# Expert weights applied on the way out of PSUM, and result rows added to X by the DMA

## The chip, the cores and the metric

One core of one Trainium2 chip runs the whole program as one launch. The metric is the time of one execution on the device in microseconds (us), as the median over several runs. TensorE (PE, with PEld for its weight loads), VectorE (DVE), ScalarE (ACT), GpSimd (POOL) and the DMA queues of SyncE (SP), ACT and POOL work side by side and meet only at semaphores.

## The reference, cut to what matters

The program is four layers of cross attention and feed-forward over X, 2048 tokens (16 tiles of 128) of 256 numbers. The change touches the feed-forward of the first layer, a mixture of 32 experts with the 6 best for each token:

```
scores = softmax(xf @ gate_w.T)                       # 2048 x 32
top_w, top_i = top_k(scores, 6)
order = argsort(e_flat);  pos = place of the pair within its expert, valid = pos < 256
xbuf[buf_idx] = xf[t_s]                               # 32 experts x 256 places
h  = silu(xb @ w1) * (xb @ w3);   ob = h @ w2         # per expert
y[t_s] += ob[buf_idx] * w_s[:, None]                  # weight w_s = the pair's score
x = x + y + shared_experts(xn)
```

The next stage, the attention of the second layer, works on the sum, tile by tile.

## The kernel before

**Routing (`choose`, `slots`, `places`).** For four groups of four tiles DVE turns the logits into probabilities (`ex`, L1720 to L1727), picks the best eight of each row into `wts` (L1730, L1733), marks the chosen experts (`hit`, L1740) and works out each pair's place. The normalised tokens `xn` are stored to DRAM as `moe_in` (L1408, on SP's queue), one row of 256 numbers for each token. `token` holds, for each of the 8192 places, the row that belongs there (L1804).

**Experts (`MoeTop6.pe`, `.dve`, `.act`, `.pool`).** There is one iteration of a loop for each expert, in a software pipeline. In iteration e, TensorE turns the 256 tokens of expert e (`expert_in`, L1588), multiplies the turned tokens of expert e-1 by w1 and w3 (`expert_up`, L1602), and multiplies h of expert e-2 by w2 (`expert_down`, L1615), in that order. DVE runs `expert_product(e-1)` (L1829) and then `expert_copy(e-2)` (L1838), which moves the 128x512 result from PSUM to the tile `oe`; ACT stores `oe` to DRAM as `moe_out` (L1907). Between these, DVE and ACT split and centre the weights of the next stage (L1250 to L1273). The queue of POOL fetches the tokens of an expert with two indirect DMAs, one for each 128 places (L1923). The tile `xe` holds R = 3 experts; the gather of expert e waits until TensorE has turned expert e-3, and `expert_in(e)` waits on the landing of both gathers of its expert. SP loads the weights of later experts as TensorE lets go of their buffers (L1441, L1447, L1448), and pieces of the next stage's weights (L1194).

```
for e in range(N_EXP):                                  # POOL
    r = e % self.R
    if e >= self.R:
        g.wait_ge(self.p_xT.sem, self.p_xT.at(e - self.R + 1))
```

**Combining (`Combine`), inside the attention after it (`Fp8Attention`).** That stage runs in steps w, eight for each tile of 128 tokens. In each step every engine does its part of some heads: TensorE scores (L3229), projections (L3280, L3273), turns (L3208, L3216), values (L3240), output (L3261); DVE the maxima `f_nmax` (L3414), the sums of squares `f_hr` (L3399), the scaling of heads `f_raw` (L3409) and the rounding; ACT the exponentials (L3492) and, behind them in its order, the copies out of PSUM (`f_PT`, L3484); POOL the powers (L3579) and the division (L3573). `prepare` comes last in each step of DVE. For tile b, POOL gathers the six result rows of each token in steps -23+j to the tile's own zero (j = 0 to 5, L1134), each into its own tile `rows[:, j]`, and DVE adds them in six steps from -20+j (L1141), in steps 4 to 1 of the eight. The moments of the tile (`MOMENTS` = -14, L3328) wait for the sixth addition. A gather waits for the addition that emptied its tile, eight steps earlier.

Of the kernel before, what the change touches and what calls it, by code (L numbers as in the profile page):

```python
# [16 lines left out]
P = 128  # L17
# [84 lines left out]
class Core:  # L102


    def __init__(self, nc, ctx, A, out):
        self.nc, self.ctx, self.A, self.out = nc, ctx, A, out
        self.sig = Signals(nc, ctx)
        self.psum = ctx.enter_context(nc.psum_tensor("bank", [P, 8 * BANK], F32))
        self.bank = [self.psum[:, i * BANK:(i + 1) * BANK] for i in range(8)]
        self.X = self.sb("X", [P, B, D])  # L110
        self.ident = self.sb("ident", [P, P])
        self.ident16 = self.sb("ident16", [P, P], BF16)
        self.ones = self.sb("ones", [P, P])
        self.half_pow = self.sb("half_pow", [P, 2 * B])
        self.zero = self.sb("zero", [P, FILL])
        self.xbuf = nc.dram_tensor("moe_in", (B * P, D), F32, kind="Internal").ap()
        self.obuf = nc.dram_tensor("moe_out", (SLOTS + 1, D), F32, kind="Internal").ap()
        self.d_x = [self.sig.claim(f"d_x{g}", 1, 16, own=True) for g in range(4)]
        self.d_const = self.sig.claim("d_const", 2, 16, own=True)
        self.d_fill = self.sig.claim("d_fill", 1, 16, own=True)  # L120
        self.d_out = self.sig.claim("d_out", 4, 16, own=True)
        self.v_const = self.sig.claim("v_const", 3, own=True)
        self.s_stage = self.sig.claim("s_stage", 0, own=True)
        self.stages = 0
        sem = lambda n: self.sig.claim(n, 0, own=True).sem
        self.dve = Chain(nc.vector, sem("dve_order"))
        self.act = Chain(nc.scalar, sem("act_order"))
        self.pool = Chain(nc.gpsimd, sem("pool_order"))
# [986 lines left out]
class Combine:  # L1115


    def __init__(self, k):
        self.k = k

# [4 lines left out]
    def signals(self):  # L1125
        claim = self.k.sig.claim
        self.d_row = [claim(f"c_d_row{j}", B, 16, own=True) for j in range(TOP_K)]
        self.v_add = claim("c_v_add", B * TOP_K, own=True)

    def gather(self, g, rows, b, j):  # L1130
        if b:
            g.wait_ge(self.v_add.sem, self.v_add.at(TOP_K * (b - 1) + j + 1))
        at = bass.IndirectOffsetOnAxis(ap=self.slot[:, b, j:j + 1], axis=0)
        g.indirect_dma_start(rows[:, j, :], None, self.k.obuf, at, bounds_check=SLOTS, oob_is_err=False).then_inc(self.d_row[j].sem, 16)  # L1134

    def add(self, v, rows, b, j):
        X = self.k.X
        v.wait_ge(self.d_row[j].sem, self.d_row[j].at(b + 1))
        if j:
            v.wait_ge(self.v_add.sem, self.v_add.at(TOP_K * b + j))  # L1140
        v.scalar_tensor_tensor(X[:, b, :], rows[:, j, :], self.wts[:, b, j:j + 1], X[:, b, :], ALU.mult, ALU.add).then_inc(self.v_add.sem, 1)  # L1141


class Fp8Weights:
# [138 lines left out]
class MoeTop6(Stage):  # L1283
# [7 lines left out]
    NG = 4  # L1291
    GROUPS = B // NG
    SI = 2 * INTER
    R, R2 = 3, 4
    LEFT, HALF = INTER - P, P // 2
    W13 = 2 * P + HALF + INTER - P
    PLACES = (0, P), (HALF, HALF + INTER - P)
# [11 lines left out]
    def allocate(self):  # L1309
        k, NG = self.k, self.NG  # L1310
        s = lambda name, shape, dt=F32: k.sb(f"m_{name}", shape, dt, self.ctx)
        self.token = s("token", [P, TILES], U32)
        self.xe = s("xe", [P, self.R, 2, D])
        self.w13 = s("w13", [P, self.R, DC, self.W13])
        with ExitStack() as c:
            s = lambda name, shape, dt=F32: k.sb(f"m_{name}", shape, dt, c)
# [1 line left out]
            self.gate = s("gate", [P, DC, N_EXP])  # L1318
            self.tri, self.ones16, self.trif = s("tri", [P, P], BF16), s("ones16", [P, P], BF16), s("trif", [P, P])
            self.expert, self.slot0 = s("expert", [P, N_EXP]), s("slot0", [P, N_EXP])  # L1320
            self.ex, self.total = s("ex", [P, NG, N_EXP]), s("total", [P, N_EXP])
# [13 lines left out]
        with ExitStack() as c:  # L1335
# [4 lines left out]
        self.rows_in = k.xbuf.rearrange("(b p) d -> p b d", p=P)  # L1340
        self.rows_out = k.obuf[0:SLOTS, :].rearrange("(e s p) d -> e p s d", e=N_EXP, p=P)
        self.signals()

    def signals(self):
        claim, G = self.k.sig.claim, self.GROUPS
        self.d_par = claim("d_par", 6, 16)
        self.d_sw = claim("d_weights", 3, 16)
        self.d_rows = claim("m_d_rows", G, 16)
# [8 lines left out]
        self.d_xe = [claim(f"m_d_xe{r}", 2 * -(-(E - r) // self.R), 16, own=True) for r in range(self.R)]  # L1357
# [11 lines left out]
    def sp(self, sp):  # L1369
        if not self.before:  # L1370
            self.load_parameters(sp)
            for g in range(self.GROUPS - 1):
                self.store_rows(sp, g)
        for t in self.tail(0, 99):
            self.before.sp_step(sp, t)
        self.store_rows(sp, self.GROUPS - 1)
        self.fp8.load_parameters(sp)
        for e in range(self.R):
            self.load_up(sp, e)
        sp.wait_ge(self.v_dn.sem, self.v_dn.at(2 * self.GROUPS))  # L1380
# [27 lines left out]
        sp.dma_start(self.rows_in[:, bs, :], self.xn[:, bs, :]).then_inc(self.d_rows.sem, 16)  # L1408

    def sp_before(self, sp, t):
        if t == 0:
# [162 lines left out]
        x.then_inc(self.p_dn.sem, 1)  # L1576

    def expert_in(self, t, e):
        i, r = e % 2, e % self.R
        ps = self.k.bank[6 + i]  # L1580
        t.wait_ge(self.d_xe[r].sem, self.d_xe[r].at(2 * (e // self.R + 1)))
# [132 lines left out]
    def choose(self, v, g):  # L1714
# [12 lines left out]
        c.mark(v.scalar_tensor_tensor(e, e, FLT_MIN, e, ALU.is_ge, ALU.mult))  # L1727
        c.after()
        for i, b in enumerate(bs):
            c.mark(v.max(wts[:, b, :], self.ex[:, i, :]))  # L1730
        c.after()
        for i, b in enumerate(bs):
            c.mark(v.max_index(self.topi[:, b, :], wts[:, b, :], self.ex[:, i, :]))  # L1733
        c.after()
        c.mark(v.tensor_copy(self.topf[:, sl, :], self.topi[:, sl, :]))
        c.after()
# [94 lines left out]
                            ALU.mult).then_inc(self.v_he.sem, 1)  # L1831

    def expert_copy(self, v, e):
        i = e % 2
        v.wait_ge(self.p_ed.sem, self.p_ed.at(e + 1))
        if e >= 2:
            v.wait_ge(self.d_oe[i].sem, self.d_oe[i].at(e // 2))
        v.tensor_copy(self.oe[:, i, :, :].rearrange("p s d -> p (s d)"), self.k.bank[4 + i][:, :]).then_inc(self.v_oe.sem, 1)  # L1838

# [71 lines left out]
    def pool(self, g):  # L1911
# [1 line left out]
            self.pool_before(g, 3)  # L1913
        self.power(g, self.GROUPS - 1)
        g.wait_ge(self.v_token.sem, self.v_token.at(1))
        g.wait_ge(self.d_rows.sem, self.d_rows.at(self.GROUPS))
        for e in range(N_EXP):
            r = e % self.R
            if e >= self.R:
                g.wait_ge(self.p_xT.sem, self.p_xT.at(e - self.R + 1))  # L1920
            for s_ in range(2):
                at = bass.IndirectOffsetOnAxis(ap=self.token[:, 2 * e + s_:2 * e + s_ + 1], axis=0)
                g.indirect_dma_start(self.xe[:, r, s_, :], None, self.k.xbuf, at, bounds_check=B * P - 1,  # L1923
                                     oob_is_err=False).then_inc(self.d_xe[r].sem, 16)

    def power(self, g, n):
# [1121 lines left out]
class Fp8Attention(Stage):  # L3048
# [274 lines left out]
    def prepare(self, v, w):  # L3323
# [1 line left out]
        c = self.k.dve  # L3325
        b = self.batch(w, self.MOMENTS)
        if b is not None:
            v.wait_ge(self.combine.v_add.sem, self.combine.v_add.at(TOP_K * (b + 1)))  # L3328
            self.moments(v, b, self.k.X[:, b, :])
        b = self.batch(w, self.SECOND)  # L3330
        if b is not None:
# [250 lines left out]
def program(nc, A, out, stages=range(8)):  # L3582
    with ExitStack() as ctx:
# [14 lines left out]
        if 1 in stages:  # L3598
            with ExitStack() as memory:
# [5 lines left out]
                with ExitStack() as rest:  # L3605
                    if first:
                        first.allocate_tail(rest)
                        spare = k.sb("spare", [P, 5120], F32, rest)
                    experts.allocate()
                    if first:  # L3610
                        flat = lambda x, dims: x.rearrange(f"p {dims} -> p ({dims})")
                        first.allocate_within(Space(flat(fp8.cut_w[:, :, :, :], "m c n").bitcast(F32), spare[:, :], flat(fp8.wkv[:, :, :], "c n"),
                                                    flat(experts.xe[:, :, :, :], "r s d")))
# [152 lines left out]
```

## Time and profile before

| | us |
|---|---|
| median of 3 runs | 2259.33 (2258.38 to 2268.91) |
| the profiled execution, its own time | 2274.26 |
| its span | 2272.5 |
| expert loop, first and last turn of tokens | starts 407.7 and 575.4 |
| attention of the second layer, in its regular part | 720 to 1280 |

The profiled execution lies 14.9 us above the median. "Busy" is the time in which an engine worked on an instruction; the releaser in square brackets is what ended an engine's idle time. Landing is the time from the issue of a DMA until its semaphore is complete.

### The profile page before, as it was taken

To read this page: it belongs to the slowest core of one execution; us is meant where nothing else is said; L and a number is where in the kernel's file an instruction comes from. 1 tells how busy PE (TensorE), PEld (TensorE's weight loads), DVE (VectorE), ACT (ScalarE), POOL (GpSimd) and SP (SyncE) were. 2 spreads that over 40 slices of the span, in tenths; PEclk is the share of its full clock that TensorE was granted. 3 is DMA by queue.
4 is the path that set the end of the run, shared out by engine and by line. 5 is a ranking of instruction groups with operands and counts; after the bars stand their busy time and mean duration, and the time that the engine had idled before them with its cause. 6 is when DMAs were issued, how large, how long until landed. Compare 5 with 4: busy or idle time off the path is not lost. (4 is left out here: it accounts for less than half of the span.)

```text
span 2272.5 us, 41321 instructions
## 1 busy us (share of the span) xinstructions
PE 1915.8 (84%) x12949; PEld 1178.3 (52%) x12949; DVE 1763.4 (78%) x4155; ACT 1355.3 (60%) x3511; POOL 959.4 (42%) x1253
## 2 busy tenths in 40 slices
PE   5999889999678999999999998598588566888888
PEld 3444355666356666666666675465244133333335
DVE  4899758464579999999999988665686797888845
ACT  0777721343168888888888886132266564577753
POOL 4444200443376566665566543232874121343210
PEclk7899859999889999999999999699599776799979
DMA  6577520678230000000001001542797310577610
GB/s 147 145 179 180 129 91 1 198 246 260 73 61 20 17 20 22 20 20 22 17 20 22 10 4 47 181 139 81 206 259 201 96 35 21 134 187 184 166 39 38
DMA packets 258319, 223.63 MB, mean 98 GB/s; under 512 B 36601, under 2 KB 237916, under 8 KB 257852
## 3 DMA queue, kind: packets, MB, share of 16 engines
q1 hardware_dynamic: 234812, 179.24, 28.8%
q0 software_dynamic: 12240, 32.39, 5.5%
q10 hardware_dynamic: 11056, 9.38, 1.3%
q8 instruction: 110, 1.80, 0.3%
q14 instruction: 101, 0.83, 0.1%
HBM read 142.50 MB, written 79.32 MB: 98 GB/s over the span
## 5 line engine op out<-in xcount | busy, mean ns | idle before, releaser
L3579 POOL TENSOR_TENSOR f_hr<-f_hr,half_pow 128x4 f32<-128x4 f32 x192 | 215.4, 1122 | 192.1 <-DVE f_hr L3399 191.6
L966 ACT ACTIVATE a_PT<-bank 128x512 f32<-128x512 f32 x384 | 214.7, 604 | 84.5 <-PE bank L720 77.6
L852 DVE TENSOR_REDUCE a_nm<-bank 128x2 f32<-128x512 f32 x384 | 243.2, 683 | 25.6 <-PE bank L713 24.2
L3492 ACT ACTIVATE f_Pm<-bank,f_nmax 128x128 f32<-128x128 f32 x512 | 183.6, 391 | 100.0 <-DVE f_nmax L3414 99.7
L713 PE MATMUL bank<-a_stack_k,a_stack_q 57*128 57x256 bf16 (+1 forms) x768 | 165.0, 300 | 80.1 <-DVE a_nm L852 45.3
L3280 PE MATMUL bank<-f_cut_w,f_zc 128*128 128x512 f16 x768 | 202.5, 388 | 14.0 <-DVE f_raw L3409 7.8
L3573 POOL TENSOR_TENSOR f_Pm<-f_Pm,f_rs 128x512 f32<-128x512 f32 x128 | 142.6, 1114 | 111.9 <-DVE f_rs L3419 111.9
L3409 DVE TENSOR_TENSOR f_raw<-bank,f_hr 128x512 f32<-128x512 f32 x192 | 131.3, 684 | 60.1 <-POOL f_hr L3579 59.4
L966 ACT ACTIVATE f_cut_w<-bank 128x512 f32<-128x512 f32 x256 | 141.7, 600 | 51.6 <-PE bank L720 41.0
L852 DVE TENSOR_REDUCE spare<-bank 128x2 f32<-128x512 f32 x256 | 162.4, 681 | 8.8 <-PE bank L713 7.4
L720 PE MATMUL bank<-a_stack_q,a_stack_k 60*128 60x256 bf16 (+1 forms) x768 | 157.7, 290 | 4.4 <-ACT a_PT L966 4.1
L3504 ACT ACTIVATE f_cb<-bank,f_rsmooth 128x128 bf16<-128x128 f32 x512 | 153.7, 431 | 5.2 <-PE bank L3240 3.5
L3216 PE MATMUL bank<-ident,f_raw 128*128 128x128 f32 x768 | 114.8, 277 | 42.4 <-ACT f_PT L3484 41.3
L713 PEld LDWEIGHTS bank<-a_stack_k,a_stack_q 57*128 57x128 bf16 (+1 forms) x768 | 59.4, 100 | 175.4 <-DVE a_nm L852 112.8
L3399 DVE TENSOR_REDUCE f_hr<-f_sq 128x4 f32<-128x516 f32 x192 | 131.2, 683 | 20.8 <-ACT f_sq L3527 20.6
L3527 ACT ACTIVATE f_sq<-bank 128x512 f32<-128x512 f32 x192 | 121.1, 631 | 43.8 <-PE bank L3273 22.1
L1923 POOL DMA_INDIRECT m_xe<-moe_in,m_token x64 | 73.6, 1150 | 168.3 <-DVE m_token L1804 81.9
L3229 PEld LDWEIGHTS bank<-f_KT,f_QT 128*128 128x128 f32 x1024 | 131.1, 194 | 20.7 <-issue 11.8
L3229 PE MATMUL bank<-f_KT,f_QT 128*128 128x128 f32 x1024 | 136.9, 277 | 0.3 <-ACT f_Pm L3492 0.3
L3240 PE MATMUL bank<-f_PT,f_Vv 128*128 128x256 f32 x512 | 132.1, 380 | 1.2 <-ACT f_cb L3504 1.2
L3273 PE MATMUL bank<-f_wkv,f_cT 128*128 128x512 f32 x256 | 123.2, 606 | 6.2 <-DMA f_cT<-in_ctx_T 5.9
L3216 PEld LDWEIGHTS bank<-ident,f_raw 128*128 128x128 f32 x768 | 91.3, 142 | 69.3 <-issue 55.9
(417 smaller groups left out, 4960.1 us busy)
## 6 DMA issues: line engine op xcount, KB each, us to landing
o<-a_sums SPq DMA_DIRECT2D x32, 512.0 KB, 4.2
cut<-a_parts SPq DMA_DIRECT2D x64, 192.0 KB, 3.9
cut<-a_parts SPq DMA_DIRECT2D x96, 128.0 KB, 3.2
m_w<-in_w SPq DMA_DIRECT2D x32, 368.0 KB, 4.6
moe_out<-m_oe ACTq DMA_DIRECT2D x32, 256.0 KB
cut<-spare SPq DMA_DIRECT2D x32, 192.0 KB, 3.5
cut<-spare SPq DMA_DIRECT2D x48, 128.0 KB, 2.6
spare<-cut SPq DMA_DIRECT2D x32, 192.0 KB, 3.6
```

The lines of the kernel that those rows point to most:

```text
L713: x = t.matmul(ps[:, n * D:(n + 1) * D], self.stack_q[rows, i, slot, n * P:(n + 1) * P], self.stack_k[rows, i, slot, :], start=True, stop= ...
L720: x = t.matmul(ps[:, n * D:(n + 1) * D], self.stack_k[rows, i, slot, n * P:(n + 1) * P], self.stack_q[rows, i, slot, :], start=True, stop= ...
L852: v.tensor_reduce(self.nm[:, g % 2, :, at % self.J, at // self.J], self.k.bank[h % 3][:, :].rearrange("p (n m) -> p n m", n=2), AX.X, ALU. ...
L966: a.activation(self.PT[:, h % 8, :, :].rearrange("p m n -> p (m n)"), self.k.bank[3 + h % 3][:, :], ACT.Exp).then_inc(self.a_exp.sem, 1)
L3216: x = t.transpose(ps[:, h * P:(h + 1) * P], self.raw[:, n % self.NRAW, h * HD1:(h + 1) * HD1], self.k.ident[:, :])
L3229: x = t.matmul(ps[:, j * P:(j + 1) * P], self.QT[:, cross, h, :], self.KT[:, cross, h // 2, :], start=True, stop=True)
L3240: x = t.matmul(self.k.bank[7][:, j * 2 * P:(j + 1) * 2 * P], self.Vv[:, cross, n * 2 + j, :], self.PT[:, u % 2, j * 2 * P:(j + 1) * 2 * P] ...
L3280: x = t.matmul(ps[:, :], self.zc[:, b % 2, j, c_, :], self.fp8.cut_w[:, m, c_, at:at + BANK], start=(m == 0 and c_ == 0), stop=(m == 1 and ...
L3492: x = a.activation(self.Pm[:, i, j * P:(j + 1) * P], ps[:, j * P:(j + 1) * P], ACT.Exp, bias=self.nmax[:, i, j:j + 1], accum_out=self.rs[: ...
L3504: x = a.activation(self.cb[:, u % self.NCB, j * P:(j + 1) * P], ps[:, j * P:(j + 1) * P], ACT.Copy, scale=self.fp8.rsmooth[:, h:h + 1])
L3573: g.tensor_tensor(pm, pm, self.rs[:, u % 3, :].unsqueeze(2).to_broadcast([P, self.HPB, P]), ALU.mult).then_inc(self.g_P.sem, 1)
L3579: g.tensor_tensor(f, f, self.k.half_pow[:, 0:self.HPB], ALU.pow).then_inc(self.g_hr.sem, 1)
```

## The change

- A second DRAM tensor, `moe_weighed`, has rows of 256 + 32 numbers: the token and its 32 probabilities. The tokens are stored to its first 256 columns; the probabilities are kept in a tile `prob`, and SP stores them to the last 32 with four DMAs (`store_prob`), each of which waits for `hit` of its group. These stand on SP's queue after the first three `load_up` and before its wait for the shared experts.
- The gathers of the tokens fetch rows of 288 numbers. The tile `xe` holds RX = 4 experts, and the gather of expert e waits for `expert_copy(e-4)`, which reads the weights from that tile.
- `expert_copy` is a multiplication by the weight of each place, broadcast over 256 columns.
- Tiles b = 0 and 1 (`PLAIN`) are still gathered to `rows` and added by DVE, now without a weight (`tensor_tensor`). For b = 2 to 15 the indirect DMA adds to X itself (`compute_op=ALU.add`), each after the landing of the one before, and DVE issues nothing; the moments wait for the landing of the sixth.
- `xe` and `spare` change size, and the first attention's tiles are laid over them in another order.

```diff
     def gather(self, g, rows, b, j):
-        if b:
-            g.wait_ge(self.v_add.sem, self.v_add.at(TOP_K * (b - 1) + j + 1))
         at = bass.IndirectOffsetOnAxis(ap=self.slot[:, b, j:j + 1], axis=0)
-        g.indirect_dma_start(rows[:, j, :], None, self.k.obuf, at, bounds_check=SLOTS, oob_is_err=False).then_inc(self.d_row[j].sem, 16)
+        if b < self.PLAIN:
+            if b:
+                g.wait_ge(self.v_add.sem, self.v_add.at(TOP_K * (b - 1) + j + 1))
+            g.indirect_dma_start(rows[:, j, :], None, self.k.obuf, at, bounds_check=SLOTS, oob_is_err=False).then_inc(self.d_row[j].sem, 16)
+            return
+        if j:
+            g.wait_ge(self.d_row[j - 1].sem, self.d_row[j - 1].at(b + 1))
+        g.indirect_dma_start(self.k.X[:, b, :], None, self.k.obuf, at, bounds_check=SLOTS, oob_is_err=False,
+                             compute_op=ALU.add).then_inc(self.d_row[j].sem, 16)
 
     def add(self, v, rows, b, j):
         X = self.k.X
+        if b >= self.PLAIN:
+            return
...
-        v.scalar_tensor_tensor(X[:, b, :], rows[:, j, :], self.wts[:, b, j:j + 1], X[:, b, :], ALU.mult, ALU.add).then_inc(self.v_add.sem, 1)
+        v.tensor_tensor(X[:, b, :], X[:, b, :], rows[:, j, :], ALU.add).then_inc(self.v_add.sem, 1)
+
+    def wait(self, v, b):
+
+        done = (self.v_add, TOP_K * (b + 1)) if b < self.PLAIN else (self.d_row[TOP_K - 1], b + 1)
+        v.wait_ge(done[0].sem, done[0].at(done[1]))
...
+    def store_prob(self, sp, g):
+        bs = slice(self.NG * g, self.NG * (g + 1))
+        sp.wait_ge(self.v_hit.sem, self.v_hit.at(g + 1))
+        sp.dma_start(self.prob_in[:, bs, :], self.prob[:, bs, :]).then_inc(self.d_rows.sem, 16)
...
     def expert_copy(self, v, e):
-        i = e % 2
+        i, weight = e % 2, self.xe[:, e % self.RX, :, D + e:D + e + 1]
...
-        v.tensor_copy(self.oe[:, i, :, :].rearrange("p s d -> p (s d)"), self.k.bank[4 + i][:, :]).then_inc(self.v_oe.sem, 1)
+        v.tensor_tensor(self.oe[:, i, :, :], self.k.bank[4 + i][:, :].rearrange("p (s d) -> p s d", s=2),
+                        weight.to_broadcast([P, 2, D]), ALU.mult).then_inc(self.v_oe.sem, 1)
...
         g.wait_ge(self.v_token.sem, self.v_token.at(1))
-        g.wait_ge(self.d_rows.sem, self.d_rows.at(self.GROUPS))
+        g.wait_ge(self.d_rows.sem, self.d_rows.at(2 * self.GROUPS))
         for e in range(N_EXP):
-            r = e % self.R
-            if e >= self.R:
-                g.wait_ge(self.p_xT.sem, self.p_xT.at(e - self.R + 1))
+            r = e % self.RX
+            if e >= self.RX:
+                g.wait_ge(self.v_oe.sem, self.v_oe.at(e - self.RX + 1))
             for s_ in range(2):
                 at = bass.IndirectOffsetOnAxis(ap=self.token[:, 2 * e + s_:2 * e + s_ + 1], axis=0)
-                g.indirect_dma_start(self.xe[:, r, s_, :], None, self.k.xbuf, at, bounds_check=B * P - 1,
+                g.indirect_dma_start(self.xe[:, r, s_, :], None, self.k.weighed, at, bounds_check=B * P - 1,
                                      oob_is_err=False).then_inc(self.d_xe[r].sem, 16)
...
-            v.wait_ge(self.combine.v_add.sem, self.combine.v_add.at(TOP_K * (b + 1)))
+            self.combine.wait(v, b)
```

## Rows read from the trace of the kernel before

**Rows 1.** The page, part 1: busy time of each engine over the span.
```profile
PE 1915.8 (84%) x12949; PEld 1178.3 (52%) x12949; DVE 1763.4 (78%) x4155; ACT 1355.3 (60%) x3511; POOL 959.4 (42%) x1253
```
**Rows 2.** Busy time by stretch: stretch, its length, engines, granted clock, DMA share, GB/s.
```profile
480.00:530.00 50.00, 50.00 (x219) 34.54 (x218) 31.39 (x43) 21.18 (x36) 22.82 (x19) 1.00 0.80 246
720.00:1200.00 480.00, 442.21 (x2714) 324.05 (x2713) 439.17 (x1113) 400.58 (x1323) 297.17 (x277) 1.00 0.08 20
```
**Rows 3.** Timeline of the expert loop: start, duration, engine, line.
```profile
482.00 0.66 PE L1588 MATMUL bank<-ident,m_xe 128*128 128x128 f32 x4
...
484.74 1.45 POOL L1923 DMA_INDIRECT m_xe<-moe_in,m_token  x1 [0.30 <-issue]
...
487.50 0.66 PE L1588 MATMUL bank<-ident,m_xe 128*128 128x128 f32 x4
...
487.60 0.69 DVE L1838 COPY m_oe<-bank 128x512 f32<-128x512 f32 x1 [1.44 <-PE bank L1615]
...
488.92 1.50 POOL L1923 DMA_INDIRECT m_xe<-moe_in,m_token  x1 [2.74 <-PE bank L1588]
...
490.73 0.99 POOL L1923 DMA_INDIRECT m_xe<-moe_in,m_token  x1 [0.30 <-issue]
```
**Rows 4.** Source line L1923: all its gathers, then two single ones.
```profile
L1923 POOL DMA_INDIRECT m_xe<-moe_in,m_token x64: 992/998/1502, 402.7 to 561.6; - x64
...
DMA to landing us min/median/max: 2.8/4.7/8.3
...
L1923 POOL DMA_INDIRECT m_xe<-moe_in,m_token x1: 998/998/998, 446.8 to 446.8; - x1
...
DMA to landing us min/median/max: 5.6/5.6/5.6
...
L1923 POOL DMA_INDIRECT m_xe<-moe_in,m_token x1: 994/994/994, 556.6 to 556.6; - x1
...
DMA to landing us min/median/max: 4.9/4.9/4.9
```
**Rows 5.** Timeline of TensorE in the attention, tile after tile: the starts after a gap.
```profile
905.08 0.63 PE L3216 MATMUL bank<-ident,f_raw 128*128 128x128 f32 x4 [0.59 <-ACT f_PT L3484]
...
917.17 1.06 PE L3216 MATMUL bank<-ident,f_raw 128*128 128x128 f32 x8 [1.24 <-ACT f_PT L3484]
...
929.89 0.63 PE L3216 MATMUL bank<-ident,f_raw 128*128 128x128 f32 x4 [0.35 <-ACT f_PT L3484]
...
937.65 1.05 PE L3261 MATMUL bank<-f_wproj,f_cb 128*128 128x256 bf16 x8 [1.06 <-DVE f_raw L3409]
...
942.74 0.63 PE L3216 MATMUL bank<-ident,f_raw 128*128 128x128 f32 x4 [0.54 <-ACT f_PT L3484]
...
953.55 0.63 PE L3216 MATMUL bank<-ident,f_raw 128*128 128x128 f32 x4 [0.59 <-ACT f_PT L3484]
```
**Rows 6.** Timeline of VectorE in the same stretch.
```profile
913.44 0.48 DVE L1141 SCALAR_TENSOR_TENSOR X<-f_rows,wts,X 128x256 f32<-128x256 f32 x1
913.84 0.68 DVE L3414 TENSOR_REDUCE f_nmax<-bank 128x4 f32<-128x512 f32 x1
...
920.62 0.69 DVE L3399 TENSOR_REDUCE f_hr<-f_sq 128x4 f32<-128x516 f32 x1 [0.36 <-ACT f_sq L3527]
```
**Rows 7.** Source line L1134: the gathers of result rows, ns, and their landing.
```profile
L1134 POOL DMA_INDIRECT f_rows<-moe_out,slot x96: 994/1092/1253, 592.9 to 1265.0; - x96
...
DMA to landing us min/median/max: 2.8/3.0/4.3
```
**Rows 8.** Groups by line, VectorE: a product that reads PSUM.
```profile
L1819 DVE TENSOR_TENSOR X<-X,bank 128x512 f32<-128x512 f32 x5 | 3.3, 683 | 4.4 <-PE bank L1574 4.4
```
**Rows 9.** Source line L1740, which writes `hit`: first and last start.
```profile
L1740 DVE TENSOR_REDUCE m_hit<-m_hot x4: 1445/1450/1486, 311.7 to 376.5; 128x128 bf16<-128x768 f32 x4
```
**Rows 10.** Busy time by stretch in two later attentions, columns as in rows 2.
```profile
1680.00:1700.00 20.00, 16.49 (x138) 8.55 (x137) 17.38 (x35) 11.24 (x24) 14.10 (x22) 0.83 0.93 260
1980.00:2000.00 20.00, 16.86 (x214) 8.26 (x214) 17.45 (x38) 15.77 (x34) 8.89 (x18) 1.00 0.76 178
```

More of the change, by code:

```diff
@@ L116, in __init__ @@
         self.xbuf = nc.dram_tensor("moe_in", (B * P, D), F32, kind="Internal").ap()
+        self.weighed = nc.dram_tensor("moe_weighed", (B * P, D + N_EXP), F32, kind="Internal").ap()
         self.obuf = nc.dram_tensor("moe_out", (SLOTS + 1, D), F32, kind="Internal").ap()
@@ L1115 @@
 class Combine:
+    PLAIN = 2
     def __init__(self, k):
@@ L1127, in signals @@
         self.d_row = [claim(f"c_d_row{j}", B, 16, own=True) for j in range(TOP_K)]
-        self.v_add = claim("c_v_add", B * TOP_K, own=True)
+        self.v_add = claim("c_v_add", self.PLAIN * TOP_K, own=True)
     def gather(self, g, rows, b, j):
-        if b:
-            g.wait_ge(self.v_add.sem, self.v_add.at(TOP_K * (b - 1) + j + 1))
         at = bass.IndirectOffsetOnAxis(ap=self.slot[:, b, j:j + 1], axis=0)
-        g.indirect_dma_start(rows[:, j, :], None, self.k.obuf, at, bounds_check=SLOTS, oob_is_err=False).then_inc(self.d_row[j].sem, 16)
+        if b < self.PLAIN:
[7 more added lines that the diff above has]
+                             compute_op=ALU.add).then_inc(self.d_row[j].sem, 16)
     def add(self, v, rows, b, j):
         X = self.k.X
+        if b >= self.PLAIN:
+            return
         v.wait_ge(self.d_row[j].sem, self.d_row[j].at(b + 1))
@@ L1293 @@
     SI = 2 * INTER
-    R, R2 = 3, 4
+    R, R2, RX = 3, 4, 4
     LEFT, HALF = INTER - P, P // 2
@@ L1312, in allocate @@
         self.token = s("token", [P, TILES], U32)
-        self.xe = s("xe", [P, self.R, 2, D])
+        self.xe = s("xe", [P, self.RX, 2, D + N_EXP])
         self.w13 = s("w13", [P, self.R, DC, self.W13])
@@ L1320, in allocate @@
             self.expert, self.slot0 = s("expert", [P, N_EXP]), s("slot0", [P, N_EXP])
-            self.ex, self.total = s("ex", [P, NG, N_EXP]), s("total", [P, N_EXP])
+            self.ex, self.total, self.prob = s("ex", [P, NG, N_EXP]), s("total", [P, N_EXP]), s("prob", [P, B, N_EXP])
             self.topi, self.topf, self.ntop = s("topi", [P, B, 8], U32), s("topf", [P, B, 8]), s("ntop", [P, B, 2])
@@ L1339, in allocate @@
             self.he, self.sge, self.oe = s("he", [P, 2, 2, CAP]), s("sge", [P, 2, 2, CAP]), s("oe", [P, 2, 2, D])
-        self.rows_in = k.xbuf.rearrange("(b p) d -> p b d", p=P)
+        weighed = k.weighed.rearrange("(b p) d -> p b d", p=P)
+        self.rows_in, self.prob_in = weighed[:, :, 0:D], weighed[:, :, D:D + N_EXP]
         self.rows_out = k.obuf[0:SLOTS, :].rearrange("(e s p) d -> e p s d", e=N_EXP, p=P)
@@ L1347, in signals @@
         self.d_sw = claim("d_weights", 3, 16)
-        self.d_rows = claim("m_d_rows", G, 16)
+        self.d_rows = claim("m_d_rows", 2 * G, 16)
         self.v_hot, self.p_who, self.v_who, self.v_token = claim("m_v_hot", G), claim("m_p_who", G + 1), claim("m_v_who", G), claim("m_v_token", 1)
@@ L1356, in signals @@
         E = N_EXP
-        self.d_xe = [claim(f"m_d_xe{r}", 2 * -(-(E - r) // self.R), 16, own=True) for r in range(self.R)]
+        self.d_xe = [claim(f"m_d_xe{r}", 2 * -(-(E - r) // self.RX), 16, own=True) for r in range(self.RX)]
         self.d_w13 = [claim(f"m_d_w13_{r}", -(-(E - r) // self.R), 16) for r in range(self.R)]
@@ L1379, in sp @@
             self.load_up(sp, e)
+        for g in range(self.GROUPS):
+            self.store_prob(sp, g)
         sp.wait_ge(self.v_dn.sem, self.v_dn.at(2 * self.GROUPS))
@@ L1578, in expert_in @@
     def expert_in(self, t, e):
-        i, r = e % 2, e % self.R
+        i, r = e % 2, e % self.RX
         ps = self.k.bank[6 + i]
-        t.wait_ge(self.d_xe[r].sem, self.d_xe[r].at(2 * (e // self.R + 1)))
+        t.wait_ge(self.d_xe[r].sem, self.d_xe[r].at(2 * (e // self.RX + 1)))
         if e < 2:
@@ L1726, in choose @@
         c.after()
-        c.mark(v.scalar_tensor_tensor(e, e, FLT_MIN, e, ALU.is_ge, ALU.mult))
+        c.mark(v.scalar_tensor_tensor(self.prob[:, sl, :], e, FLT_MIN, e, ALU.is_ge, ALU.mult))
         c.after()
-        for i, b in enumerate(bs):
-            c.mark(v.max(wts[:, b, :], self.ex[:, i, :]))
+        for b in bs:
+            c.mark(v.max(wts[:, b, :], self.prob[:, b, :]))
         c.after()
-        for i, b in enumerate(bs):
-            c.mark(v.max_index(self.topi[:, b, :], wts[:, b, :], self.ex[:, i, :]))
+        for b in bs:
+            c.mark(v.max_index(self.topi[:, b, :], wts[:, b, :], self.prob[:, b, :]))
         c.after()
@@ L3607, in program @@
                         first.allocate_tail(rest)
-                        spare = k.sb("spare", [P, 5120], F32, rest)
+                        spare = k.sb("spare", [P, 4096], F32, rest)
                     experts.allocate()
@@ L3611, in program @@
                         flat = lambda x, dims: x.rearrange(f"p {dims} -> p ({dims})")
-                        first.allocate_within(Space(flat(fp8.cut_w[:, :, :, :], "m c n").bitcast(F32), spare[:, :], flat(fp8.wkv[:, :, :], "c n"),
-                                                    flat(experts.xe[:, :, :, :], "r s d")))
+                        first.allocate_within(Space(flat(fp8.cut_w[:, :, :, :], "m c n").bitcast(F32), flat(experts.xe[:, :, :, :], "r s d"),
+                                                    spare[:, :], flat(fp8.wkv[:, :, :], "c n")))
                         plan.append(first)
```

## The prediction, made before the changed kernel ran

> **What bounds the kernel now.** I read the page's busy table first: TensorE is busy for 84% of the span and VectorE for 78% [rows 1], so neither is the bound everywhere, and each stage has to be read by itself. The change works in two. The view of busy time by stretch shows the expert loop with TensorE busy for 50.00 of 50 us at the full clock, VectorE for only 31.39, and the DMA engines at 0.80 [rows 2]: TensorE alone sets the time there, and everything else has slack as long as it arrives on time. In the attention after it TensorE is busy for 442.21 of 480 us and VectorE for 439.17 [rows 2]; the two share the bound, and the timeline says who waits for whom. In the eight steps that one tile takes, behind the gap at 905.08, TensorE stands still five times, 1.24 + 0.35 + 1.06 + 0.54 + 0.59 = 3.8 us in all, four times for a copy of ScalarE and once for VectorE [rows 5]. ScalarE's copies stand behind exponentials that wait for VectorE's maxima, and the maxima come straight after the addition that closes VectorE's step (913.44, then 913.84) [rows 6]. So additions on VectorE do reach TensorE, in this stage only.
>
> **Part 1, the additions leave VectorE: a gain.** There are 16 x 6 = 96 additions of 0.48 us [rows 6]; 14 of 16 tiles lose theirs, 84 in all. The instruction behind one starts 0.40 us after it (913.44 to 913.84) [rows 6], so what is freed is 84 x 0.40 = 33.6 us, or 2.4 us for each tile. How much of this reaches the end I take from the gaps [rows 5]. The addition at 913.44 delays the maxima of the step with the 1.24 gap: 0.40 back. The next one stands in a step where VectorE is ahead and waits 0.36 for ScalarE at 920.62 [rows 6]: nothing back. The third stands before the gap of 0.35: 0.35 back. The fourth and fifth stand before 1.06 and 0.54: 0.40 each. The sixth is followed by a step without a gap, but VectorE's lead is carried to the gap of 0.59: I give it half, 0.2. That is 1.7 us for each tile, 14 x 1.7 = **-24 us**. The ends are -33.6 (all of it; the gaps, 3.8, would hold it) and 0 (TensorE finds another late partner each time). The twelve additions that stay lose their weight operand and keep their time.
>
> **Part 2, the DMA adds.** POOL issues the same 96 indirect DMAs, 1.09 us each [rows 7]. New is that gathers j = 1 to 5 of 14 tiles, 70 in all, wait for the landing of the one before. They are issued one step apart, and a tile takes 953.55 - 905.08 = 48.5 us (the same wait, one tile apart) [rows 5], a step an eighth of it, 6.1 us. A plain gather lands in 3.0 us, at most 4.3 [rows 7]. An adding one isn't in the trace; from both sides, 3.0 (no dearer) and twice that, 6.0 (it reads X as well), both end within a step. Behind the waiting gather on POOL's queue stand the next step's power and division, which VectorE and TensorE need, so beyond 6.1 us it would hurt; up to there it costs nothing. Its moments are taken four steps after the sixth gather: hidden by 24 us.
>
> **Part 3, the expert's tokens are fetched later: a loss.** Before, the gather of expert e was let go by the turning of expert e-3, three iterations ahead. Now it waits for `expert_copy(e-4)`. `expert_down(e-4)` is the last work of iteration e-2, so the copy runs at the start of iteration e-1, and only that one iteration lies between the gather's release and `expert_in(e)`. There are four buffers, but the release comes two iterations later. Working it out:
> - One iteration is 487.50 - 482.00 = 5.50 us [rows 3].
> - The copy runs from 487.60 to 488.29; the turning that releases POOL today ends at 488.16. So POOL starts 0.1 later than now. It now starts its second gather at 490.73, 3.23 after the iteration's start [rows 3]; that becomes 3.33.
> - The second gathers of this phase, ten from 446.8 (5.6 us) to 556.6 (4.9 us), have a median landing of 4.9 [rows 4].
> - Landed: 3.33 + 4.9 = 8.2 us after the end of iteration e-2, where 5.5 would do. TensorE waits 2.7 us.
> - The phases alternate. In the other one the second gather starts at 484.74, 2.74 after the start [rows 3]; with the 0.1 and the median of all landings, 4.7 [rows 4], it is in after 7.5 us. Two iterations then take the longer of 5.5 + 8.2 = 13.7 and 5.5 + 7.5 = 13.0, against 11.0 now. So the gap of 2.7 falls once in two experts, and the other gather has 0.7 to spare.
> - Twelve pairs (experts 8 to 31): 12 x 2.7 = 32.4. One of them meets the 2 MB load of the next stage, where a landing takes up to 8.3 [rows 4]: 3.4 more. Experts 4 to 7 have the short phase twice: 2 x (13.0 - 11.0) = 4.0. Sum **+40 us**.
>
> The ends: with the shortest landing, 2.8 [rows 4], the wait is 3.33 + 2.8 - 5.5 = 0.6, 14 times: +9. With 5.6 [rows 4] it is 3.4: 12 x 3.4 + 3.4 + 4 = +48. I stay at 4.9, since the gathers keep their place in the iteration and with it the loads and the store they share the engines with; rows of 288 numbers instead of 256 speak for more, the idle 2.7 us for less. The share of busy DMA, 0.80 now [rows 2], would go down by 11.0/13.7.
>
> A landing has a price in the Trainium skill too ("DMA: Bandwidth & Descriptors", section on the anatomy of one DMA on the gpsimd path): about 2.0 us plus the bytes at 436 GB/s, by which 147 KB would take an estimated 2.3 us, the wait would be 0.1 and the whole part some 2 us. By that, the trace disagrees under this load: the shortest of its 64 landings is 2.8, and those of this phase stand near 5.
>
> **Part 4, the rest, at nothing.** `expert_copy` reads PSUM with a second operand: 0.683 us for this size [rows 8] against 0.69 now [rows 3]. The four stores of probabilities stand on SP's queue ahead of its wait for the last shared addition, which VectorE issues after `hit` of the last group anyway, so they hold up nothing there. That `hit` is written at 376.5 + 1.45 = 378 [rows 9], 25 us before the first gather at 402.7 [rows 4]; this slack is the cover, and without it the first gather would be late by one landing, some 5 us. The new destinations of `choose` and the layout of the first attention change no instruction's size.
>
> **Sum.** -24 + 40 + 0 = +16 us. On the profiled execution's own time that is 2274.3 + 16 = 2290; it lies 14.9 above the median, and against the median of 2259.3 I forecast **2275 us**.
>
> **The rivals.**
> - *The gathers land early, not slower.* If landings in the loop come down to 2.8, the smallest of 64 [rows 4], because TensorE's waiting empties the queues, the loop loses 9 us and the attention gains 24 to 33.6: -15 to -25, some 2239. It decides at a landing of 3.9: 3.33 + 3.9 - 5.5 = 1.7, 14 x 1.7 = 24, the gain of part 1. For it speak that the gap comes before the iteration and thins the traffic; against it that the loads are issued at the same places in an iteration as before. The skill's page named above gives a like outcome by its price. Chance 0.14.
> - *The clock falls in the gaps.* In one later attention TensorE is busy for 16.49 of 20 us and has a mean granted clock of 0.83, so that it spends a third of the time at 1.2 GHz and the rest at 2.4, in another for 16.86 at 1.00, all at 2.4 [rows 10]. The expert loop would have 11.0 of 13.7, as low a share as these. At 0.83 its 28 iterations, 154 us, take 154/0.83 - 154 = 31 us more: +47, 2306. Chance 0.17.
> - *The freed VectorE brings nothing*, since ScalarE (400.58 of 480 [rows 2]) or the powers of POOL hold TensorE instead: +40, 2299. Chance 0.09.
> - *Adding DMAs land late.* At 8.3 us, the largest landing of any gather [rows 4], each of 70 waits holds POOL 2.2 us, 154 us; POOL is idle for 38% of the stage [rows 2] and would swallow about half, so +77 on top: 2352. Chance 0.06.
> - *It cancels*, the waits shrinking to 1.7 us a pair: 2259. Chance 0.12.
> - The forecast as worked out: 0.42, mostly between 2262 and 2292.
>
> **How the numbers follow.** A measurement of this kernel can tell about 0.5%, 11 us, from no change. Slower by more: two thirds of the forecast (0.29), most of the clock's fall (0.16), nothing freed (0.09), late adding (0.06), 0.60. Faster by more: nearly all of early landings, 0.13. Within: the rest, 0.27. The range leaves out the late adding and the outer part of early landings, and reaches to the clock's case: 2240 to 2312.
>
> **What would show it.** In the changed profile L1588 would wait for the DMA of the tokens some 14 times, 2 to 3 us each, and TensorE's share in 480 to 530 fall to about 0.8; POOL would wait for `expert_copy`, not for the turn. In the attention one tile would take 46.8 us instead of 48.5, L1141 stand 12 times, and TensorE's gaps be halved. Wrong would be: no wait at L1588 (part 3), a tile of 48 us or more (part 1), or POOL waiting for landings at L1134 (part 2).

## The result, and the profile after

The changed kernel takes 2315.0 us (median of 4 runs, 2304.0 to 2320.4) beside 2260.5 for the kernel before, also of 4 runs. The ratio of their runs is 1.0215, with a 95% interval of 1.0183 to 1.0248, which on 2260.5 is +49 us; the medians differ by 54.5. Medians and ratios, here and below, leave out executions in a slower state of the chip; the profile of the run with the late release alone is of one and is read for its expert loop only. The profiled execution took 2320.4 us, its span 2318.6, 46.1 more than before. Two source lines give the place: the turns of tokens, which stand once in every iteration of the expert loop, and the output additions of the attention, once in every second step (L1613 and L3470 of the changed kernel, L1588 and L3444 before): durations in ns, first and last start.

```profile
L1613 PE MATMUL bank<-ident,m_xe x128: 272/273/477, 406.1 to 637.3; 128*128 128x128 f32 x128
...
L3470 DVE SCALAR_TENSOR_TENSOR X<-bank,f_ws,X x64: 468/477/485, 763.8 to 1457.2; 128x256 f32<-128x256 f32 x64
```
The same rows of the kernel before:
```profile
L1588 PE MATMUL bank<-ident,m_xe x128: 272/273/473, 407.7 to 575.8; 128*128 128x128 f32 x128
...
L3444 DVE SCALAR_TENSOR_TENSOR X<-bank,f_ws,X x64: 470/473/485, 698.7 to 1409.0; 128x256 f32<-128x256 f32 x64
```

| part of the profiled span, us | before | after | |
|---|---|---|---|
| up to the first turn of tokens | 407.7 | 406.1 | -1.6 |
| expert loop, first to last turn | 168.1 | 231.2 | +63.1 |
| from there to the first output addition (run-in of the attention) | 122.9 | 126.5 | +3.6 |
| first to last output addition | 710.3 | 693.4 | -16.9 |
| the rest | 863.5 | 861.4 | -2.1 |
| span | 2272.5 | 2318.6 | +46.1 |

The loop loses 63 us and the attention gives back 13. Busy time by stretch, with the columns of [rows 2], for the changed kernel:

```profile
480.00:530.00 50.00, 41.47 (x158) 29.16 (x158) 21.49 (x29) 14.94 (x25) 13.98 (x13) 0.86 0.58 172
...
760.00:1240.00 480.00, 456.18 (x2807) 334.78 (x2807) 425.35 (x1082) 413.43 (x1364) 338.42 (x287) 1.00 0.13 21
```
Where [rows 2] has TensorE busy for 50.00 of 50 us at the full clock with 219 matmuls, it is now busy for 41.47, the mean granted clock is 0.86, so part of the stretch runs at 1.2 GHz, the lower of its two levels, and only 158 matmuls get done. In the attention TensorE's share has gone up, from 442.21 of 480 to 456.18. The waits of the loop (who waited for whom, total, times, longest) name the cause:

```profile
POOL m_xe L1949 <- DVE m_oe L1863: 151.6, 28, 10.4
...
PEld bank L1613 <- DMA m_xe<-moe_weighed,m_token: 46.4, 16, 5.8
...
PE bank L1613 <- DMA m_xe<-moe_weighed,m_token: 39.3, 15, 5.4
```
POOL stands ready and waits 28 times for the copy of a result, which is what lets go of a buffer now, and TensorE waits for the DMA that POOL then issues. The timeline shows one round of it, to be read beside [rows 3]:

```profile
520.79 1.11 PE L1613 MATMUL bank<-ident,m_xe 128*128 128x128 f32 x4 [2.80 <-DMA m_xe<-moe_weighed,m_token]
...
527.68 0.66 PE L1613 MATMUL bank<-ident,m_xe 128*128 128x128 f32 x4
527.79 0.69 DVE L1863 TENSOR_TENSOR m_oe<-bank,m_xe 128x512 f32<-128x512 f32 x1 [1.43 <-PE bank L1640]
...
529.25 1.24 POOL L1949 DMA_INDIRECT m_xe<-moe_weighed,m_token  x1 [7.27 <-DVE m_oe L1863]
530.79 1.00 POOL L1949 DMA_INDIRECT m_xe<-moe_weighed,m_token  x1 [0.30 <-issue]
...
535.91 0.66 PE L1613 MATMUL bank<-ident,m_xe 128*128 128x128 f32 x4 [2.67 <-DMA m_xe<-moe_weighed,m_token]
541.41 0.66 PE L1613 MATMUL bank<-ident,m_xe 128*128 128x128 f32 x4
```
The last two rows are one iteration without a wait, 5.50 us as before. The iteration from 527.68 to 535.91 holds a wait of 2.67: the second gather is issued at 530.79, lands 5.1 us later by the row of its source line, 535.9, and TensorE starts. From 520.79 to 527.68 there is no wait at all, yet the iteration takes 6.89: its four turns take 1.11 us in place of 0.66, which is TensorE at the lower of its two clock levels. So the 63 us are waits and clock. Busy time over the whole loop, before and after, gives a first division:

```profile
407.70:575.80 168.10, 166.26 (x720) 115.81 (x721) 89.98 (x148) 66.12 (x115) 69.50 (x61) 0.98 0.77 241
...
406.10:637.30 231.20, 191.90 (x720) 133.66 (x721) 87.97 (x148) 66.13 (x115) 64.65 (x61) 0.86 0.59 180
```
The same 720 matmuls keep TensorE busy for 25.6 us longer, and its idle time goes from 1.8 to 39.3 us, +37.5. The experiments have to show what causes either.

### The profile page after: what moved, and what is told of

Read it like the earlier page. It is cut to its first block and busy times, and to the rows that moved or that the text cites. A ratio compares the mean times of both kernels' runs of the same rounds, so it can differ in the third digit from the quotient of the medians.

```text
span 2318.6 us, 41171 instructions
## 1 busy us (share of the span) xinstructions
PE 1932.6 (83%) x12949; PEld 1195.2 (52%) x12949; DVE 1720.3 (74%) x4071; ACT 1354.7 (58%) x3511; POOL 997.6 (43%) x1253
## 3 DMA queue, kind: packets, MB, share of 16 engines
q0 software_dynamic: 20304, 33.44, 7.2%
## 5 line engine op out<-in xcount | busy, mean ns | idle before, releaser
L3605 POOL TENSOR_TENSOR f_hr<-f_hr,half_pow 128x4 f32<-128x4 f32 x192 | 221.7, 1155 | 160.8 <-DVE f_hr L3425 159.6
L1949 POOL DMA_INDIRECT m_xe<-moe_weighed,m_token x64 | 68.7, 1074 | 244.2 <-DVE m_oe L1863 151.6
L853 DVE TENSOR_REDUCE m_xe<-bank 128x2 f32<-128x512 f32 x256 | 162.2, 679 | 8.8 <-PE bank L714 7.2
L3553 ACT ACTIVATE f_sq<-bank 128x512 f32<-128x512 f32 x192 | 121.1, 631 | 45.5 <-PE bank L3306 22.7
L1143 POOL DMA_INDIRECT X<-moe_out,slot x84 | 137.4, 1636 | 21.3 <-issue 12.7
```

The source lines that it names most:

```text
L853: v.tensor_reduce(self.nm[:, g % 2, :, at % self.J, at // self.J], self.k.bank[h % 3][:, :].rearrange("p (n m) -> p n m", n=2), AX.X, ALU. ...
L1143: g.indirect_dma_start(self.k.X[:, b, :], None, self.k.obuf, at, bounds_check=SLOTS, oob_is_err=False, compute_op=ALU.add).then_inc(self.d ...
L3605: g.tensor_tensor(f, f, self.k.half_pow[:, 0:self.HPB], ALU.pow).then_inc(self.g_hr.sem, 1)
```

## The experiments

Theory A: the gather waits for `expert_copy(e-4)`, lands 2.7 us late for every second expert (some 40 us), and the clock falls because of the gaps (some 23 us). Rivals: the loop is slow because of what it computes and moves now (longer rows, a product in place of a copy); or the clock falls for a reason of its own. For the attention: the additions' relief, less what the adding DMAs cost on POOL, or nothing of that.

**One more token buffer.**
```diff
-    R, R2, RX = 3, 4, 4
+    R, R2, RX = 3, 4, 5
```


> The changed kernel with five token buffers instead of four, so that a gather is let go one iteration earlier. Theory A (the late release costs 40 us of waits and the clock's fall that follows from them 23 us): a gather has 11.0 us where it needs 8.2, the waits at the turning of tokens go, the granted clock in the loop is back at 1.00, the loop's turns span 168 us instead of 231, and the whole takes some 2315 - 63 = 2252 us, a little under the kernel before. Rival B (the longer rows of 288 numbers and the product with a broadcast weight slow the loop): the waits shrink at most in part and the kernel stays above 2290.

Measured: 2258.5 us (10 runs) beside 2262.2, ratio 0.9967 (0.9936 to 0.9998), 6 us above the 2252 that was expected. The loop spans 169.8 us, and busy time by stretch has it back:
```profile
480.00:530.00 50.00, 50.00 (x221) 34.72 (x220) 30.66 (x42) 23.03 (x38) 19.84 (x18) 1.00 0.82 245
```
TensorE is busy throughout at 2.4 GHz, and the DMA engines at 0.82 move the longer rows beside the rest. The wait at the turn of tokens shrinks from 39.3 us to 3.5, nearly what it was before (1.8). One buffer takes away waits and clock loss together, so both hang on the release; the longer rows and the product cost the loop 1.7 us at most (169.8 and 168.1).

**The waits filled.** Twenty turns of the identity on TensorE ahead of the wait, for even experts from 4 on; what they write is overwritten by the turns behind them. The wait for the tokens moves behind them.
```diff
+        for _ in range(20 if e >= 4 and e % 2 == 0 else 0):
+            t.transpose(ps[:, 0:P], self.k.ident[:, :], self.k.ident[:, :])
         t.wait_ge(self.d_xe[r].sem, self.d_xe[r].at(2 * (e // self.RX + 1)))
```


> The changed kernel with twenty extra turns of the identity on TensorE ahead of the wait for the tokens of each even expert from 4 on, some 2.2 us that fit into the wait of 2.7. Theory A says that the waits alone cost 40 us and that the other 23 us are TensorE at the lower clock: with the waits filled, the granted clock in the loop is 1.00, the loop spans 208 to 212 us instead of 231, and the whole takes some 2295. Rival C (the clock falls for another reason, or the 23 us are longer landings): clock and loop stay as they are or get longer, 2315 or more.

Measured: 2300.3 us (4 runs), ratio to before 1.0152 (1.0087 to 1.0217), where 2295 was expected; the loop spans 209.6 us. One round on TensorE's timeline:
```profile
492.81 2.41 PE L1611 MATMUL bank<-ident 128*128 128x128 f32 x20
495.80 0.65 PE L1615 MATMUL bank<-ident,m_xe 128*128 128x128 f32 x4 [0.58 <-DMA m_xe<-moe_weighed,m_token]
```
and busy time in the stretch and in the whole loop:
```profile
480.00:530.00 50.00, 48.58 (x251) 35.70 (x250) 24.06 (x33) 18.38 (x30) 15.40 (x14) 1.00 0.65 197
...
404.80:614.40 209.60, 200.50 (x999) 147.26 (x1000) 88.01 (x149) 66.14 (x115) 64.74 (x61) 0.98 0.65 199
```
The fill ends 0.58 us before the tokens land, so the gather is as late as ever, but the clock stays at 1.00 and the turns behind it take 0.65 us. The loop does more work and is 21.6 us shorter; of the whole kernel the times don't show it beyond doubt, since the intervals of 1.0152 and 1.0215 overlap. With the mean clock of the loop back at 0.98, as before, the loop's 63.1 us divide into 231.2 - 209.6 = 21.6 for the clock and 209.6 - 168.1 = 41.5 for the waits; by busy and idle time above it was 25.6 and 37.5. The rival of another reason for the clock falls.

**Late release alone, in the kernel before.** Four token buffers, rows of 256 numbers, no weights. The tile `xe`, its semaphores and the wait in `expert_in` go by RX in the same way, and `spare` is smaller to make room; of the edit only the release is printed.
```diff
...
-            r = e % self.R
-            if e >= self.R:
-                g.wait_ge(self.p_xT.sem, self.p_xT.at(e - self.R + 1))
+            r = e % self.RX
+            if e >= self.RX:
+                g.wait_ge(self.v_oe.sem, self.v_oe.at(e - self.RX + 1))
...
```


> The kernel before, unchanged but for the token buffers: four of them, and the gather of an expert waits for the copy of the result four experts back. Rows have 256 numbers and no weight is applied. Theory A: the same waits at the same experts, the loop's turns span 225 to 231 us instead of 168, the whole 2260 + 60 = 2320 us. Rival B (row length and product make the loss): less than 2280 us.

Measured: 2315.0 us (3 runs), ratio 1.0229 (1.0158 to 1.0300), which on 2262 is 36 to 68 us. The profiled execution took 2342.4, 27 above that median; 7.8 us of what it takes more than the profile before lie behind the output additions, 61.7 in the loop. The loop spans 229.8 us at a granted clock of 0.87, and the wait is the same as in the changed kernel to 0.3 us:
```profile
PEld bank L1588 <- DMA m_xe<-moe_in,m_token: 46.1, 16, 6.0
```
Of what the change does in the loop only the release is in this kernel, and its loop has 61.7 of the 63.1 us: rows and product are out of it.

**All additions on VectorE, four buffers.**
```diff
-    PLAIN = 2
+    PLAIN = 16
```


> The changed kernel with all sixteen tiles gathered to the row tiles and added by VectorE, weights still applied in the expert loop. If the DMA's adding brings the attention 13 us net, as the spans of the stage say (first to last output addition 693 instead of 710, run-in 4 longer), this takes 2315 + 13 = 2328 us, and one tile of the attention 48.5 us again. If it brings nothing, 2315; if it were worth the 24 us forecast, 2339.

Measured: 2326.9 us (6 runs), ratio 1.0283 (1.0230 to 1.0337), 12 us over the changed kernel by the medians and 15 by the ratios (1.0283 and 1.0215 of 2260), as the value of 13 said. First to last output addition 708.4 us, the run-in 121.3. The loop's code is that of the changed kernel, but in this profile the loop spans 223.4 us and not 231.2:
```profile
398.20:621.60 223.40, 182.79 (x720) 127.00 (x721) 87.96 (x148) 66.14 (x115) 64.65 (x61) 0.90 0.61 186
```
Idle time is the same to 1.3 us (40.6 and 39.3), busy time 9.1 us less. So what the clock takes differs from one execution to the next: by busy time 16.5 us here and 25.6 there, and the 21.6 of the filled kernel, from one pair of profiles, has this width too.

**All additions on VectorE, five buffers.** Both edits. What is left of the change are weights, longer rows and the stores of probabilities.

> Five token buffers and all additions on VectorE: what is left of the change is the weighting on the way out of PSUM, the stores of probabilities and the longer rows. Theory A prices these at nothing: the loop 168 to 170 us, the attention 708 to 710, the whole as before, 2258 to 2264. Against five buffers with the DMA's adding it should be 13 us slower. Rival: a cost of 5 us or more for the longer rows.

Measured: 2265.3 us (9 runs) beside 2265.2, ratio 1.0009 (0.9978 to 1.0040): no change, as expected, though the median lies 1 above the 2258 to 2264 that was named. Loop 169.3 us, output additions 709.3. The weighting is free within 0.4% either way. Over five buffers with the adding DMAs it is 0.4% by the ratios, 9 us where 13 were expected, taken on two different chips.

**Nobody adds.** Five buffers; for tiles 2 to 15 the gathers are plain ones, each after the landing of the one that went to the same row tile a tile of tokens earlier, and the routed experts are missing from the output of those tiles.
```diff
-        if j:
-            g.wait_ge(self.d_row[j - 1].sem, self.d_row[j - 1].at(b + 1))
-        g.indirect_dma_start(self.k.X[:, b, :], None, self.k.obuf, at, bounds_check=SLOTS, oob_is_err=False,
-                             compute_op=ALU.add).then_inc(self.d_row[j].sem, 16)
+        g.wait_ge(self.d_row[j].sem, self.d_row[j].at(b))
+        if b == self.PLAIN:
+            g.wait_ge(self.v_add.sem, self.v_add.at(TOP_K * (b - 1) + j + 1))
+        g.indirect_dma_start(rows[:, j, :], None, self.k.obuf, at, bounds_check=SLOTS, oob_is_err=False).then_inc(self.d_row[j].sem, 16)
```


> Five token buffers, and for tiles 2 to 15 the result rows are gathered plainly to the row tiles and added by nobody, neither DMA nor VectorE, so the routed experts are missing from those tiles. It frees VectorE as the change does, without the adding DMA's 1.63 us on POOL (a plain one takes 1.09) and without its chained waits. Theory A (the gain of 17 to 18 us is what VectorE's relief is worth, and POOL's longer issues and waits cost a few us of it): first to last output addition below 692, at 684 to 690, and the run-in back to 123 us; the whole 5 to 12 us under the kernel with five buffers. Rival B (POOL's time is hidden): the same as with five buffers, 692 and 2257.

Measured: 2245.0 us (10 runs), ratio 0.9921 (0.9895 to 0.9947). The run-in takes 120.6 us, first to last output addition 691.1, where Theory A had 684 to 690. To see where this differs from adding DMAs, here is the time from one tile to the next, between starts of the instruction that ends a tile's normalisation (L3345 before, L3371 after), worked out from the timelines:

```
                               tile 0-1  1-2   2-3 to 13-14       14-15
before                         25.2     35.7   48.3 to 48.5       48.2
all additions on VectorE, RX=5 25.1     35.6   48.1 to 48.3       48.0
after (adding DMAs)            27.3     39.6   46.7 to 47.4       46.5
nobody adds, RX=5              25.1     35.3   46.9               46.6
tile 2 on VectorE, RX=5        25.1     36.4   46.7 to 47.6       46.6
```
In the regular part, nobody adding gains next to nothing over the DMA adding, 1.5 us over 13 tiles: 46.9 us is what VectorE's relief can bring, and POOL's longer issue is hidden there. In the run-in the adding DMAs cost 2.1 + 3.9 = 6.0 us, and with plain gathers nothing. (The two profiles with five buffers alone have 27.4 + 39.4 and 27.4 + 37.7 there, so 4.2 to 6.0 more than before.) Theory A held for the run-in and was wrong for the regular part, where it had POOL costing something.

**Tile 2 on VectorE.**
```diff
-    PLAIN = 2
+    PLAIN = 3
```


> Five token buffers, and tile 2 is added by VectorE as tiles 0 and 1 are. Tile 2's adding gathers fall in the run-in, where steps are shorter than the 4.0 us in which one lands, and POOL waits for them. Theory A: these waits are the 3.6 us that the run-in got longer; with tile 2 on VectorE the run-in is back near 123 us and the whole 1 to 3 us faster than five buffers alone, the regular part unchanged at 692. Rival: the run-in stays at 126, and its length comes from elsewhere.

Measured: 2248.4 us (10 runs) beside 2265.2, ratio 0.9937 (0.9907 to 0.9967). It is 7 us less than five buffers alone by the ratios (0.9967, on another chip), where 1 to 3 were expected. The run-in is at 120.9 us and takes 25.1 + 36.4 in the table. The source lines of the adding gathers say what stood in the run-in before; first the changed kernel, with the idle time of POOL just before them, and the landing:
```profile
L1143 POOL DMA_INDIRECT X<-moe_out,slot x84: 1609/1629/1783, 682.0 to 1313.7; - x84
...
  issue: 12.7, 58
  DMA X<-moe_out,slot: 6.8, 7
...
DMA to landing us min/median/max: 3.8/4.0/4.7
```
then the one with tile 2 on VectorE:
```profile
L1143 POOL DMA_INDIRECT X<-moe_out,slot x78: 1630/1643/1687, 656.2 to 1248.4; - x78
...
  DMA X<-moe_out,slot: 2.2, 3
```
The waits for landings go down from 6.8 us (4.1 and 6.0 in the two profiles with five buffers alone) to 2.2, and the first adding gather is issued 78.9 us after the loop's last turn in place of 44.7. The waits are not the whole of it: those of tile 2's gathers in the changed kernel are 0.82 + 1.32 + 1.38 = 3.5 us. Its six issues are also 0.54 us longer each than plain ones, 3.2 us in all, and both this kernel and the one where nobody adds take away waits and longer issues together. Which of the two costs the run-in its 6.0 us was not parted.

**The two best once more, on one chip.**

> Five token buffers once more, on the same chip as its variant with tile 2 on VectorE, to tell the two and the kernel before apart. By the spans of the profiles (loop +1.6, run-in +6.0, thirteen tiles -18.7 us against before, and 2 to 3 us less after and ahead of them) it should take 0.4 to 0.8% less than before.

> The same with tile 2 added by VectorE, on the same chip. Without the 6 us of the run-in it should take 0.6 to 1.1% less than before, and 3 to 6 us less than five buffers alone; rival: the run-in's gain is lost elsewhere and the two are equal.

Measured beside 2263.3 us: five buffers alone 2249.7 us (8 runs), ratio 0.9937 (0.9910 to 0.9964); with tile 2 on VectorE 2247.6 us (9 runs), ratio 0.9934 (0.9908 to 0.9959). Both beat the kernel before, by what was expected of each. Between them lie 2.1 us where 3 to 6 were expected, inside either interval: the profiles show the run-in 3.2 us shorter (124.3 and 121.1), but the rival, that the whole gains nothing by it, isn't ruled out by the times. The best kernel found is the change with RX = 5, PLAIN being 2 or 3: 0.6% faster than before here, 0.3% where RX = 5 was first measured. The two profiles of five buffers alone, one and the same kernel, reach the first turn of tokens at 404.9 and 394.3 us; a few us between two kernels are no more than such differences between executions.

## Why the prediction was right, and where it was off

The direction and the mechanism were right: the gain on VectorE is real and smaller than the loss in the loop. The size was too small. 2275 was forecast and 2315 measured, 3 above the upper end of 2312; by the ratio it is 2309, inside. It is inside only because the range was drawn up to the clock's case; every term that was off was off in the same direction (by the divisions of the experiments 1.5 + 21.6 + 5.3 + 6.0 = 34 us, beyond the forecast of +16).

- **Part 3, the late release.** This was the working that carried the forecast, +40 us, and the waits measured 37.5 to 41.5. The gap of every second expert was put at 2.7; the timeline has 2.67 and 2.80, and by the same view the 14 gaps run from 1.6 to 5.4 and sum to 37.6 us, 2.7 in the mean, the 5.4 beside the 2 MB load, where 2.7 + 3.4 = 6.1 had been put. The choice of a landing of 4.9, by the place of the gather among the other transfers, was right (4.9 and 5.1 for the two gathers behind the 2.67). Of its ten gathers the median leaves out an eleventh, at 534.67, whose 8.1 the working prices apart; with it the median is 5.0. By the price of the Trainium skill ("DMA: Bandwidth & Descriptors", section on the anatomy of one DMA on the gpsimd path), an estimated 2.3 us, the part would have been 2 us; under this load the trace disagrees. The kernel before, with this release alone, and the changed one, with one buffer more, show it from both sides.
- **The clock was kept in a rival, at a chance of 0.17.** It is the step that made the forecast too low. It was priced at +31 us and measured 21.6 (16.5 and 25.6 by busy time in two profiles), and it came on top of the waits, as that rival had it: 2306, 3 to 9 us from what was measured. The row that spoke for it was there, 16.49 of 20 us busy at 0.83 [rows 10], and so was one against it; a loop that was to be busy for 80% of its time deserved more than 0.17. The filled kernel ties it to the gaps.
- **Part 1, VectorE's relief, -24 us.** One tile takes 47.0 us in the mean in place of 48.4, 1.4 less, where 1.7 was forecast. The gaps of TensorE in one tile of the changed kernel are these (those of before are [rows 5]):

```profile
1010.98 0.63 PE L3242 MATMUL bank<-ident,f_raw 128*128 128x128 f32 x4 [0.58 <-ACT f_PT L3510]
1022.77 1.06 PE L3242 MATMUL bank<-ident,f_raw 128*128 128x128 f32 x8 [0.93 <-ACT f_PT L3510]
1042.45 1.05 PE L3287 MATMUL bank<-f_wproj,f_cb 128*128 128x256 bf16 x8 [0.66 <-DVE f_raw L3435]
...
1057.92 0.63 PE L3242 MATMUL bank<-ident,f_raw 128*128 128x128 f32 x4 [0.57 <-ACT f_PT L3510]
```
  The gaps of 0.35 and 0.54 are gone, 1.24 is 0.93, 1.06 is 0.66 and 0.59 is 0.57: 0.35 + 0.54 + 0.31 + 0.40 + 0.02 = 1.6, close to the working, addition by addition, except that the sixth bought nothing at the gap of 0.59 and the fifth more than its own 0.40. VectorE now waits longer for ScalarE's squares, which points to TensorE's own work (456 of 480 us) as the limit:
```profile
1026.22 0.69 DVE L3425 TENSOR_REDUCE f_hr<-f_sq 128x4 f32<-128x516 f32 x1 [0.99 <-ACT f_sq L3553]
```
  where [rows 6] has a wait of 0.36. The larger slip was the count: tile 2's additions fall in the run-in, where VectorE isn't the bound, so 13 tiles gain, not 14. By the table that is 18.7 us.
- **Part 2, the adding DMA, at nothing.** In the regular part that held: its landing, 4.0 us, lies between the bounds of 3.0 and 6.0 and under a step of 6.1. It failed in the run-in, where steps take 25.2/8 = 3.2 to 35.7/8 = 4.5 us, and a landing of 4.0 doesn't fit the shorter ones: there the adding DMAs cost 6.0 us. The step length had been taken from the regular part for all 14 tiles. It also took for granted that issuing costs POOL what a plain gather costs (1.09 us, and measured 1.63), and how much of the 6.0 us is this, and how much the landings, stays open. The sign that was named for this part, POOL waiting for landings at the adding gathers, did show, with 6.8 us.
- **Part 4** held: `expert_copy` takes 0.69 us with the weight, as without it, and the kernel with all additions on VectorE and five buffers has a ratio of 1.0009.

By parts, +41.5 + 21.6 - 18.7 + 6.0 = +50 us, beside +46.1 in the profiled spans and +49 by the ratio; of the difference to the spans, 3.7 us lie ahead of the loop and behind the attention. The table of tiles and that of spans cut the attention at other places: -18.7 + 6.0 = -12.7 there, -16.9 + 3.6 = -13.3 here.

## What to carry to other kernels

When a buffer gets a second reader at the end of a pipeline, ask when its refill is issued, not only how many buffers there are: here four buffers instead of three went with a release two iterations later, and what counts is the time from the start of the iteration that releases to the landing (8.2 us) against the iterations left for it (one, 5.5). A stage whose TensorE was never idle can pay twice for a new gap, once as the wait and once, at the lower clock, as work; here the second bill was four tenths to seven tenths of the first. Price a moved transfer with the landing at its own place in the traffic, and check a run-in by its own step length.

## What the runs showed of the hardware

- An indirect DMA that adds 128 rows of 1 KB to SBUF keeps POOL for 1.63 us, a plain one for 1.09 [rows 7], and lands in 4.0 us in place of 3.0. The software queue's packets rose from 12240 to 20304, 96 more for each of the 84 adding DMAs; the bytes (32.39 and 33.44 MB) rose only by the longer rows of tokens, and the kernels with weights in which no DMA adds have 12240 packets and the same 33.44 MB:

```profile
q0 software_dynamic: 20304, 33.44, 7.2%
```
  The Trainium skill ("Collectives: The Full Stack", on why ReduceScatter is half of AllGather) says of the reduce step of a collective that the add is slower for its second source read, with a descriptor of its own, and not for the adding. More packets come with the adding here too, but three times as many and not twice: in 100 us of the attention (1000 to 1100 in both profiles) the queue has 1872 in place of 624. That the packets are what cost POOL its 0.54 us was not tried.
- Waits of 1.6 to 5.4 us, 2.7 in the mean, in rounds of two iterations (15.1 us from 520.79 to 535.91) took the mean granted clock of the loop from 0.98 to 0.86, in another execution to 0.90. Twenty turns of the identity in each of them, work that nobody needs, brought it back to 0.98 and won back 21.6 us of the loop.
- A multiplication by a weight broadcast over 256 columns costs VectorE the same 0.69 us as the plain copy out of PSUM (medians 0.690 and 0.692).
